# Dense key tiles, statistics by sequence, early folding, a two-tensor floor, and the gate on ScalarE and GpSimd in a two-branch transformer kernel

## What is computed

```
q, k, v = split(shift(x) @ Wqkv)                  # 16 heads of 64
q = rotary(q / max(|q|, 1e-12) * qs);  k = rotary(k / max(|k|, 1e-12) * ks)
x = x + softmax(mask(8 * q @ k.T)) @ v @ Wo
xn = layernorm(shift(x)) * g + b
a, gate = split(xn @ W1 + b1)                     # 341 each
x = x + (a * gelu(gate)) @ W2 + b2
```

## Time and profile before

| | |
|---|---|
| median of 3 runs | 4503.34 us (4500.78 to 4506.68) |
| the profiled execution | 4507.01 us |
| its span | 4505.2 us, 98224 instructions |
| PE busy | 4176.7 us, 93% |
| PE weight loads busy | 2719.6 us, 60% |
| DVE busy | 4086.5 us, 91% |
| ACT busy | 2795.8 us, 62% |
| POOL busy | 2811.6 us, 62% |
| mean granted TensorE clock | 0.992 of full |

### The profile page before, as it was taken

The page is one execution under the profiler, slowest core; times in us unless marked ns, Lnnn a source line. Parts: engine busy times, 40 slices in busy tenths (PEclk is TensorE's granted clock), DMA queues, the critical chain, the costliest instruction groups (busy, mean ns, idle before and its releaser), DMA issues. The chain is left out here.

```text
span 4505.2 us, 98224 instructions
## 1 busy us (share of the span) xinstructions
PE 4176.7 (93%) x35048; PEld 2719.6 (60%) x35048; DVE 4086.5 (91%) x5503; ACT 2795.8 (62%) x4035; POOL 2811.6 (62%) x4591
## 2 busy tenths in 40 slices
PE   5999999999979999999999999999999999999997
PEld 3555555555456666666666666666666666666664
DVE  5888788888779999999999999999999999999995
ACT  4666666666545666656666666666666666666663
POOL 3555555555556666666666666666666666676663
PEclk9999999999989999999999999999999999999998
DMA  1000000000010000100011000100001000001000
GB/s 54 3 6 5 3 3 5 5 3 3 14 39 15 16 16 20 36 19 16 15 30 28 16 17 15 32 27 16 17 19 38 17 15 17 19 18 37 16 16 14
DMA packets 173509, 81.44 MB, mean 18 GB/s; under 512 B 109120, under 2 KB 168512, under 8 KB 172224
## 3 DMA queue, kind: packets, MB, share of 16 engines
q1 hardware_dynamic: 173248, 78.08, 6.3%
HBM read 48.56 MB, written 16.91 MB: 15 GB/s over the span
## 5 line engine op out<-in xcount | busy, mean ns | idle before, releaser
L572 POOL TENSOR_TENSOR pn<-es,rden 128x1024 f32<-128x1024 f32 x192 | 366.7, 1910 | 691.7 <-DVE rden L903 691.7
L666 ACT ACTIVATE y<-ps 128x1024 f32<-128x1024 f32 x384 | 372.3, 1021 | 506.0 <-PE ps L1109 506.0
L556 POOL TENSOR_TENSOR t<-t,ardn 128x1024 f32<-128x1024 f32 x256 | 485.1, 1895 | 305.1 <-DVE ardn L788 304.8
L657 ACT ACTIVATE t<-ps,anm,srn 128x512 f32<-128x512 f32 x512 | 392.9, 771 | 272.3 <-DVE anm L797 272.3
L576 POOL TENSOR_TENSOR t<-t 128x1024 f32<-128x1024 f32 x192 | 454.8, 2369 | 87.8 <-DVE t L855 87.8
L855 DVE TENSOR_TENSOR t<-ps,tabl 128x512 f32<-128x512 f32 x768 | 491.0, 681 | 0.0
L853 DVE TENSOR_TENSOR t<-ps,tabl 128x1024 f32<-128x1024 f32 x384 | 467.1, 1216 | 15.9 <-ACT sq L682 13.0
L578 POOL TENSOR_TENSOR t<-t 128x1024 f32<-128x1024 f32 x192 | 453.1, 2360 | 2.1 <-DVE t L855 2.1
L957 DVE TENSOR_TENSOR qn<-t,rn 128x2048 f32<-128x2048 f32 x192 | 438.1, 2282 | 4.9 <-POOL rn L388 4.9
L913 DVE TENSOR_REDUCE ss<-sq 128x32 f32<-128x2048 f32 x192 | 437.0, 2276 | 0.0
L986 PEld LDWEIGHTS ps<-cst,qn 128*128 128x128 f32 x3072 | 350.0, 141 | 114.4 <-issue 58.6
(11 more groups left out here) (136 smaller groups left out, 8863.0 us busy)
## 6 DMA issues: line engine op xcount, KB each, us to landing
tokens_dram<-x SPq DMA_DIRECT2D x96, 128.0 KB
xs<-tokens_dram SPq DMA_DIRECT2D x192, 64.0 KB, 1.8
xw<-tokens_dram SPq DMA_DIRECT2D x192, 64.0 KB, 1.9
xsh<-x SPq DMA_DIRECT2D x48, 128.0 KB
xsh<-x SPq DMA_DIRECT2D x48, 127.0 KB
wm<-in_l_wqk SPq DMA_DIRECT2D x3, 1024.0 KB, 5.0
wv<-in_l_wv SPq DMA_DIRECT2D x6, 512.0 KB, 3.8
wo<-in_l_wo SPq DMA_DIRECT2D x6, 512.0 KB, 4.6
```

Of the source, the lines that this page charges most:

```text
L556: nc.gpsimd.tensor_tensor(eA[:, v], eA[:, v], ardn[:, v].unsqueeze(2).to_broadcast([P, 2, SEQ]), ALU.mult).then_inc(a_pn, 1)
L657: e = act.activation(eA[:, j, h], bank(j % 2 * 2 + h), ACT.Exp, bias=anm[:, j, h:h + 1], scale=srn[:, a % 2, j, h:h + 1], accum_out=aden[: ...
```

## The change

Five edits:

1. **Dense keys.** `kpad` goes; `kT` holds the transposed keys as 8 pairs x 544 columns, two heads on the two halves of the partitions, with no zeros but the first window. One ACT copy fills a block. The scores are 64 products on 64 rows, 64 keys each, instead of 32 on 128 rows with 128 keys. Heads are stored in another order (all even, then all odd), so the folded weights are taken in that order.
2. **Statistics by sequence.** Each sequence's statistics are taken one sequence ahead within attention, and the inverse root is Newton's on POOL. Loads are reordered, and each engine waits for what it needs alone.
3. **Early folding.** The first layer's `wv`, `wo` are loaded at the start into tiles that attention doesn't use, and folded while attention drains.
4. **Floor.** L915 becomes the maximum of two tensors; the half goes into the Newton constants (3, 12, 768), and the factor 8192 that comes of it is divided out in the rotation tables.
5. **Gate.** ACT writes `a + b1` from PSUM to `fh`, and POOL multiplies it by the gelu.

The diff, cut to its core:

```diff
@@ sync: order of the loads @@
-            sp.dma_start(cst[:], consts[:, 0:CST]).then_inc(s_ld, 16)
...
+            load_tokens(0, s_x0)
+            sp.dma_start(cst[:], consts[:, 0:CST]).then_inc(s_ld, 16)
+            sp.dma_start(wqkL[0], a_wqk).then_inc(s_wa, 16)
+            sp.dma_start(wv[:].rearrange("p h d -> p (h d)"), a_wv).then_inc(s_wa, 16)
+            sp.dma_start(boutb[:], a_bout.partition_broadcast(P)).then_inc(s_ld, 16)
+            sp.dma_start(sc[:], a_logit.partition_broadcast(P)).then_inc(s_ld, 16)
+            sp.dma_start(wo[:].rearrange("p h d -> p (h d)"), a_wo).then_inc(s_wa, 16)
+            for b in range(1, NB):
+                load_tokens(b, s_x)
...
+            sp.dma_start(wv0, l_wv[0]).then_inc(s_wv0, 16)
+            sp.dma_start(wo0, l_wo[0]).then_inc(s_wv0, 16)
...
                 if s.turn_of(-1, 2):
                     store_sums(NB - 1)
-                    layer_value_output(0)
-                    sp.wait_ge(s_accd, 16 * NB)
...
+                    if s.first:
+                        sp.wait_ge(s_accd, 16 * NB)
                     layer_projection(s.l + 1, 1 - s.v)
@@ gpsimd @@
+            for k, value in enumerate(ROOT_CONSTS):
+                nc.gpsimd.memset(root_const[:, k], value).then_inc(s_avg, 1)
+            nc.gpsimd.memset(floor_const[:], NORM_FLOOR).then_inc(s_avg, 1)
...
+                        if a == 3 and not last:
+                            if j == 0:
+                                pool.wait_ge(a_xg, b + 2)
+                            newton(pool, a_xr, b + 1, frn[:], fhalf[:], frt[:], range(3 * j, 3 * j + 3))
...
-            nc.gpsimd.memset(kpad[:], 0.0).then_inc(s_zero, 1)
+            nc.gpsimd.memset(kT[:, :, 0:WIN], 0.0).then_inc(s_zero, 1)
+
+            def gate(n, c):
+                pool.wait_ge(f_g, n * NC + (c + 1))
+                pool.wait_ge(f_v, n * NC + (c + 1))
+                nc.gpsimd.tensor_tensor(fh[0:CH[c], c], fh[0:CH[c], c], fg[0:CH[c], :], ALU.mult).then_inc(f_h, 1)
...
                     pool.wait_ge(l_gs, t + 4)
-                    newton(pool, l_rs, t + 3, rn[:], ss[:], rt[:])
+                    newton(pool, l_rs, t + 3, rn[:], ss[:], rt[:], scaled=True)
+                if c == 0 and s.ffn(2):
+                    gate(s.f2, 2)
+                if c >= 2 and s.ffn(1):
+                    gate(s.f1, c - 2)
                 if c == 0 and s.ffn(1):
@@ scalar @@
+                        if last and a == PAIRS:
+                            act.wait_ge(s_m, j + 1)
+                            act.activation(mhL[0][:, j * 4:(j + 1) * 4].rearrange("p h d -> p (h d)"), bank(j),
+                                           ACT.Copy).then_inc(s_msb, 1)
...
                                bias=b1s[0:CH[c], NC + c:NC + c + 1]).then_inc(f_g, 1)
+                if c == 0:
+                    past(act, f_o, n)
+                act.activation(fh[0:CH[c], c], bank(6)[0:CH[c], :], ACT.Identity,
+                               bias=b1s[0:CH[c], c:c + 1]).then_inc(f_v, 1)
...
-                    act.activation(*keys(0, (c + 2) % NU), ACT.Copy)
-                    act.activation(*keys(1, (c + 2) % NU), ACT.Copy).then_inc(l_kT, 1)
+                    u = (c + 2) % NU
+                    act.activation(kT[:, :, WIN + u * P:WIN + (u + 1) * P], pool2.rearrange("p (a c) -> p a c", a=PAIRS),
+                                   ACT.Copy).then_inc(l_kT, 1)
@@ vector @@
+            def token_guess(b):
+
+                dve.wait_ge(a_mv, b + 1)
+                nc.vector.tensor_scalar(fhalf[:], agg[:, :, 1], EPS, 0.5, ALU.add, ALU.mult).then_inc(a_hv, 1)
+                dve.wait_ge(a_hv, b + 1)
+                nc.vector.tensor_scalar(frn[:].bitcast(I32), fhalf[:].bitcast(I32), -0.5, float(0x5F3759DF - (1 << 22)),
+                                        ALU.mult, ALU.add).then_inc(a_xg, 1)
...
+                        if a == 2 and j == 1 and not last:
+                            token_statistics(b + 1)
+                        if a == 2 and j == 3 and not last:
+                            token_guess(b + 1)
...
-            def gate(n, c):
-                dve.wait_ge(f_g, n * NC + (c + 1))
-                if c == 0:
-                    past(dve, f_o, n)
-                nc.vector.scalar_tensor_tensor(out=fh[0:CH[c], c], in0=bank(6)[0:CH[c], :], scalar=b1s[0:CH[c], c:c + 1],
-                                               in1=fg[0:CH[c], :], op0=ALU.add, op1=ALU.mult).then_inc(f_h, 1)
...
-                    nc.vector.tensor_scalar(ss[:], ss[:], NORM_FLOOR, 0.5, ALU.max, ALU.mult).then_inc(l_fl, 1)
+                    nc.vector.tensor_tensor(ss[:], ss[:], floor_const[:], ALU.max).then_inc(l_fl, 1)
@@ tensor @@
+            def fold_first(q):
+
+                pe.wait_ge(s_wv0, 32)
+                pe.wait_ge(a_e, NB * STEPS - (q < 2))
+                products(q, wv0.rearrange("p (h d) -> p h d", h=PAIRS), wo0.rearrange("p (h d) -> p h d", h=PAIRS), bank(q))
...
+                        if last and a == PAIRS:
+                            fold_first(j)
...
-                past(pe, f_h, n * NC + c)
+                past(pe, f_v, n * NC + c)
...
-                        for w in range(NW):
-                            key0 = u * P + w * WIN
-                            m = nc.tensor.matmul(pool1[w * WIN:(w + 1) * WIN, a * 2 * KEYS:(a + 1) * 2 * KEYS],
-                                                 qT[:, a, w * WIN:(w + 1) * WIN], kpad[:, 2 * a:2 * a + 2, key0:key0 + KEYS],
-                                                 start=False, stop=True, skip_group_check=True)
+                        for odd in range(2):
+                            rows = slice(odd * DH, (odd + 1) * DH)
+                            for w in range(NW):
+                                key0 = u * P + w * WIN
+                                m = nc.tensor.matmul(pool1[w * WIN:(w + 1) * WIN, odd * 512 + a * KEYS:odd * 512 + (a + 1) * KEYS],
+                                                     qT[rows, a, w * WIN:(w + 1) * WIN], kT[rows, a, key0:key0 + KEYS],
+                                                     start=False, stop=True, skip_group_check=True)
```

More of the change, by code:

```diff
@@ L149, in build @@
         agg = sb("agg", [P, NU, 2])
[L150 to L153, removed]
+        gap = sb("gap", [P, NU])
         ass = sb("ass", [P, NU * 4])
@@ L317, in build @@
         s_out = sem("s_out")
[L319 to L323, removed]
         def layers(eng, turn):
@@ L378, in heads, with newton @@
             return ap.rearrange("p (h d) -> p h d", h=n)
-        def newton(pool, done, count, root, half, tmp, steps=range(RS_POOL)):
-            const = c15[:, 0:root.shape[-1]]
+        def newton(pool, done, count, root, half, tmp, steps=range(RS_POOL), scaled=False):
             for step in steps:
+                const = root_const[:, step // 4] if scaled else c15[:, 0:root.shape[-1]]
                 to, a, b, op = ((tmp, root, root, ALU.mult), (tmp, tmp, half, ALU.mult),
@@ L388, in newton @@
                 nc.gpsimd.tensor_tensor(to, a, b, op).then_inc(done, 1)
[L390 to L407, removed]
         block = ctx.enter_context(nc.Block())
@@ L743, in _ @@
                 dve.wait_ge(a_st, b + 1)
-                nc.vector.memset(rt[:, 0:NU], 0.0)
+                nc.vector.memset(gap[:], 0.0)
                 for u in range(NU):
@@ L865, in statistics @@
                 dve.wait_ge(f_st, n + 1)
-                nc.vector.memset(artmp[:, 0:NU], 0.0)
+                nc.vector.memset(gap[:], 0.0)
                 for k in range(NU):
@@ L929, in turn @@
                                         pn[:].rearrange("p (h n k) -> p n h k", h=H, n=2)).then_inc(l_pT, 1)
-                if c == 0 and s.ffn(2):
-                    gate(s.f2, 2)
                 if c == 1 and s.ffn(2):
@@ L942, in turn @@
                     ffn_bias(s.l)
-                if c >= 2 and s.ffn(1):
-                    gate(s.f1, c - 2)
                 if s.has(2):
@@ L965, in _, with products @@
         def _(pe):
-            def fold(n, q):
-                pe.wait_ge(s_wvo, (n + 1) * 32)
+            def products(q, a, b, to_bank):
                 for h in range(H):
@@ L972, in fold @@
                         rows = slice(h % 2 * DH, (h % 2 + 1) * DH)
[L973 removed]
+                        m = nc.tensor.matmul(to_bank[:, to % 4 * DIM:(to % 4 + 1) * DIM], a[rows, h // 2], b[rows, h // 2],
                                              start=True, stop=True)
                 m.then_inc(s_m, 1)
+            def fold(n, q):
+                pe.wait_ge(s_wvo, n * 32)
+                products(q, wv, wo, ps_x)
+            def fold_first(q):
+                pe.wait_ge(s_wv0, 32)
+                pe.wait_ge(a_e, NB * STEPS - (q < 2))
+                products(q, wv0.rearrange("p (h d) -> p h d", h=PAIRS), wo0.rearrange("p (h d) -> p h d", h=PAIRS), bank(q))
             def project(src, i, v, pool):
@@ L1115, in ffn_transpose @@
                 pe.wait_ge(f_xn, n + 1)
```

(2 more changed lines are left out.)

98 lines of the change are left out of this document (53 added, 45 removed).

## The result

The changed kernel took 4591.24 us (median of 4 runs, 4588.0 to 4599.58) against 4504.9 for the kernel before: ratio 1.0196, 95% interval 1.0183 to 1.0209, slower by 86 us. The forecast was 4535, range 4450 to 4590: the measured time lies 1.2 us above the range. The direction was right, the size was not. The profiled execution took 4589.7 (span 4587.9), with a mean granted clock of 0.979 (before 0.992).

A forecast was written before the change was run, and what follows sets the result against it. Three nearly level chains (PE, the root through POOL and DVE, DVE's transpose to ACT's exponential) bound a layer turn. Terms 39 + 5 + 26 − 5 − 12 − 23 + 10 − 8 = +32 on 4507 gave 4539, by the median 4535 us; range 4450 to 4590.

The forecast's parts named there:

- Gate in c=2, c=3: Layer turns c=2, c=3: POOL's gate product blocks DVE's L957, +0.48 in each of 82 turns, +39 us.
- Gate in c=0: Layer turns c=0: gate is over before L957, DVE's gain is lost, +0.1 × 47 = +5 us.
- In c=1: Layer turns c=1: POOL arrives late, L915 waits longer for its rotation add, +0.6 × 43 = +26 us.
- Floor: L915 in the layers: still ends when POOL's L578 does; -5 us, between 0 and -10.
- Dense keys: Score block in the layers: 1.95 to 1.2 us, paying only where PE ends last, 20 × -0.6 = -12 us.
- Start and attention: Before the layers: PE starts near 14 instead of 37.34, -23 us; statistics inside attention add +10.
- Handover: From attention's last sum to the first projection: early loads and folds bring L980 forward, -8 us.
- Rival (a): Turns c=2, c=3: no collision at L957, 4455 us by the median; chance 0.31 including the case of ineffective edits.
- (b): Whole kernel: start, handover and folds give 20 more, or half the collision; near 4503 us; chance 0.08.
- (c): Score block in the layers: limited by entry of records, 3.8 us, PE +1.9, kernel 4810 us; chance 0.08.
- floor of about 25: PE's small products: skill page's minimum ns start to start, by which the score block would be 3.2 us.

The follow-up runs named there:

- e1: Changed kernel with the gate back on DVE; dense keys, floor, statistics and early folds stay: 4551.8 us, ratio 1.0107.
- e2: Changed kernel with keys as before; gate on ACT and POOL, floor, statistics and early folds stay: 4573.56 us, ratio 1.0162.
- e10: e1 with PE's loop over the sequences written out, the other engines' loops kept: 4481.23 us, ratio 0.9955.
- e6: e3 plus the two-tensor floor with scaled Newton steps: 4498.35 us, ratio 0.9993.
- e11: Changed kernel with PE's loop over the sequences written out: 4574.5 us, ratio 1.0162.
- e12: e3 with PE's loop written out, as control for e10: 4493.12 us, ratio 0.9977.
- e3: Kernel before plus only statistics by sequence, reordered loads and early folding; keys, gate and floor as before: 4496.0 us, ratio 0.9986.
- e14: Changed kernel with PE's loop written out and DVE's feed-forward statistics behind the transpose in c=0; gate left on ACT and POOL: 4589.82 us, ratio 1.0190.
- e16: e2 with POOL's gate product taken twice in c=2 and c=3, the first into an unused tile: 4586.25 us, ratio 1.0180.
- e7: e1 with the two mask products done three times instead of once in c=0: 4541.16 us, ratio 1.0087.

## Why the prediction missed

- **Gate in c=2, c=3** (+39): right in mechanism, +47 measured (e1, e2). The turn takes 16.10 for 15.97, since the product lasts 1.27 and not the earlier trace rows's 1.07: both its operands are full tensors, while `frn` in L591 is four elements spread out. That this is the reason for the difference is argued, not shown.
- **Gate in c=0** (+5): 0.0 in e2. **In c=1** (+26): +22.3 in e2. In the changed kernel it showed as +5.7, since longer c=0 turns let POOL catch up (L934 takes 0.77 there in the median, between 0.27 and 2.37; in e2 2.11) and short scores save PE 0.40 in c=1 (e10: 16.41 for 16.81).
- **Floor** (-5): nothing (e6).
- **Dense keys** (-12): the step that failed. The score block was near (1.49; I had 1.2), and in c=1 and c=3 they gave more than forecast once the loop is written out, 18 us in e10; with the loop as it is they gave 6 (e1). I had not counted that c=1 is a turn that PE bounds (the fold turns c=2 gave 0.38 each, 16.38 for 16.76, of the 0.6 forecast). The term was taken as a gain only "where PE ends last", so c=0 stood at nothing. Two things were left out there. First, what a longer wait does: the clock is halved in 27 of 48 turns, which costs 35.0 us in the changed kernel, 26.8 in e1, 31.4 in e11 and 22.2 in e10. Second, the 128 records more in each turn: I priced what PE executes, not what it must be sent. In c=0 the jump with its fetch costs 57 us without the gate (e1 against e10) and 29 with it (after against e11), in both some 8 less by the control e12; the whole time fell by 70.6 and 16.7, in the control by 2.9.
- **Start and attention** (-13 in sum): -11.4. **Handover** (-8): -9.6, but 7.7 of it comes with the dense keys, by the smaller clearing, not with the folds (e3).

The terms measured alone don't add up to the whole, since gate and dense keys overlap (102.5 us together, 65.6 and 69.7 alone). In the changed kernel itself the rows are -21.0 + 50.1 + 5.7 + 25.2 + 21.5, and 1.2 behind the last turn's start, 82.7 in all, by which the two profiled executions differ. The forecast was 32. Of the 51 that are missing, c=0 is 45; c=1 came 20 lower, c=2 and c=3 8 higher, and the -12 and -5 of dense keys and floor didn't show as gains. Rival (a) fell (L972 takes 3.35, and e1 gives the 47 back), (b) with it, (c) fell (1.49 us). No rival of mine had the fetch or the clock.

## What to carry to other kernels

An edit that splits the same work into more instructions has a second price, in the program's size: compare the instruction queue's packets of the first pass through the loop with those of a later pass, and where the later passes show any, write the loop out or keep it short. Shortening work ahead of a wait buys nothing and can cost: here 0.46 us less of scores made a wait of 1.68 one of 2.0, and in 19 of 48 turns of e1 the clock was halved behind it, in none before. On the port that DVE and POOL share, count how many POOL instructions can stand ahead of one of DVE's (one), and how many of DVE's in a row can meet one each (two in e14).

## What was not expected of the hardware

- Instructions come in packets of 16.4 KB. A PE loop of 1193 matmuls and weight loads stayed loaded, one of 1707 was loaded again at each pass, and its first transpose after the jump waited 1.2 to 1.7 us in layers 1 to 4 of e1, in layer 0 up to 1.5 and 2.8 in a row. The same turns written out waited 2.4 us in sum, for 42.0 (e10).
- 64 products of 64 rows, 32 columns and 64 elements, 128 records, take 1.49 us: 11.6 ns a record, under the floor of about 25 that the prediction quotes; the measurement decides.
- DVE and POOL take turns at the shared port by instruction (e16, e14): with two of POOL's products in a row, DVE was held by one only.
- The same wait of 1.97 us is followed by the full clock in one turn and by half of it in another (e10). Waits of 1.72 to 1.82 were followed by half of it in four turns of e7, waits of 1.78 to 1.84 by the full clock throughout in e2.
